# A gated cross-attention block on one core: gate and up of two token blocks by Strassen's seven products

## The reference

```python
x = x + tanh(g_xattn[0]) * xattn(layernorm(x), ctx, ctx, Wq, Wk, Wv, Wo)   # x: (2, 2048, 512), ctx: (2, 77, 512), 16 heads of 32, causal mask
x = x + tanh(g_ffn[0]) * ffn(layernorm(x))

def ffn(x):                       # HIDDEN = 1536, weights are int32 in -127..127, times 1/127
    gate = einsum('bsd,hd->bsh', x, wg)
    up = einsum('bsd,hd->bsh', x, wu)
    return einsum('bsh,dh->bsd', silu(gate) * up, wd)
```

## Time and profile before

| | |
|---|---|
| median of 3 runs | 936.83 us (935.4 to 937.76) |
| the profiled execution's own time | 934.25 us |
| its span | 932.0 us |
| mean granted TensorE clock | 0.996 of full speed |
| TensorE busy | 899.7 us, 97% |
| VectorE, ScalarE, GpSimd busy | 514.3, 349.9, 316.1 us |

### The profile page before, as it was taken

How to read it: one execution, slowest core, us unless ns; L and a number is a source line. 1 busy time by engine, 2 the same in 40 slices (tenths; PEclk the granted TensorE clock), 3 DMA queues, 4 the chain that set the end, 5 groups by cost and what they waited for, 6 DMA issues and landing times.

```text
span 932.0 us, 12820 instructions
## 1 busy us (share of the span) xinstructions
PE 899.7 (97%) x4281; PEld 745.7 (80%) x4281; DVE 514.3 (55%) x918; ACT 349.9 (38%) x999; POOL 316.1 (34%) x273
## 2 busy tenths in 40 slices
PE   5979999999999999999999999999999999999997
PEld 3757888888888887788888888888888888888886
DVE  4767867777776758587255244254262352442641
ACT  3565565556565657353033022122132131231230
POOL 5456544626272624134033032042141131231230
PEclk9989999999999999999999999999999999999999
DMA  6433424251421236730200200200100200100001
GB/s 218 125 99 107 136 65 133 76 166 49 144 79 68 79 102 195 233 115 1 71 19 12 79 0 11 79 0 23 68 0 23 68 0 34 56 0 34 12 0 47
DMA packets 48704, 65.83 MB, mean 71 GB/s; under 512 B 7328, under 2 KB 20128, under 8 KB 48672
## 3 DMA queue, kind: packets, MB, share of 16 engines
q1 hardware_dynamic: 48384, 65.41, 21.7%
q10 hardware_dynamic: 288, 0.00, 0.0%
HBM read 48.29 MB, written 16.79 MB: 70 GB/s over the span
## 4 chain that ended last, share of the span: by engine, by line
PE 84%; POOL 4%; DVE 4%; SPq 3%; issue 2%; ACT 2%; DMA 1%; POOLq 0%; ACTq 0%; DVEq 0%
PE psum L1183 61%; PE psum L1412 19%; POOL xs L488 3%; PE psum L1217 3%; SPq L378 2%; PE psum L1203 2%; POOL e L502 1%; DVE pT L828 1%; DMA wq_stage<-wq_t 1%; ACT pT L633 1%; DVE aT L844 1%; ACT aT L650 1%; ACT e L662 1%; DVE den L882 0%; SPq L310 0%
## 5 line engine op out<-in xcount | busy, mean ns | idle before, releaser
L1183 PE MATMUL psum<-xT,w_gu 128*128 128x512 f32 x1536 | 349.6, 389 | 0.0
L1183 PEld LDWEIGHTS psum<-xT,w_gu 128*128 128x128 f32 x1536 | 288.3, 188 | 59.9
L577 POOL TENSOR_TENSOR hT<-hid,hT 128x512 fp32r<-128x512 f32 x96 | 124.4, 1296 | 392.8 <-ACT hT L783 392.8
L778 ACT ACTIVATE th<-psum 128x512 f32<-128x512 f32 x96 | 57.5, 599 | 363.3 <-PE psum L1183 363.3
L1412 PE MATMUL psum<-w_d,hT 128*128 128x512 f32 x768 | 178.1, 391 | 0.0
L1412 PEld LDWEIGHTS psum<-w_d,hT 128*128 128x128 f32 x768 | 143.1, 188 | 29.1
L1068 DVE SCALAR_TENSOR_TENSOR th<-th,psum 128x512 f32<-128x512 f32 x96 | 66.0, 687 | 161.8 <-ACT th L778 161.1
L502 POOL TENSOR_TENSOR e<-e,rden 128x616 f32<-128x616 f32 x64 | 77.9, 1218 | 163.1 <-DVE rden L884 133.8
L1183 PE MATMUL psum<-xT,wq 128*128 128x512 f32 x384 | 96.4, 404 | 3.0 <-POOL xT L494 2.9
L1183 PE MATMUL psum<-wo,aT 128*128 128x512 f32 x384 | 95.9, 399 | 0.0
L1082 DVE SCALAR_TENSOR_TENSOR x<-psum,gate_ffn,x 128x512 f32<-128x512 f32 x32 | 24.0, 751 | 123.9 <-PE psum L1412 123.9
(11 more groups left out here) (81 smaller groups left out, 778.8 us busy)
## 6 DMA issues: line engine op xcount, KB each, us to landing
x_ln<-x SPq DMA_DIRECT2D x32, 256.0 KB, 4.6
x_res<-x SPq DMA_DIRECT2D x32, 256.0 KB, 3.9
x_mid<-x_res SPq DMA_DIRECT2D x32, 256.0 KB, 2.1
x<-x_mid SPq DMA_DIRECT2D x8, 1024.0 KB, 5.6
out<-x SPq DMA_DIRECT2D x32, 256.0 KB, 2.0
xs<-x_t SPq DMA_DIRECT2D x28, 256.0 KB, 3.4
raw<-w_gate_t SPq DMA_DIRECT2D x12, 256.0 KB, 3.5
raw<-w_up_t SPq DMA_DIRECT2D x12, 256.0 KB, 4.6
```

What stands on the lines that cost most here:

```text
L577: nc.gpsimd.tensor_tensor(hT[:, 1, m, :], hid[:, m % 2, :], hT[:, 0, m, :].bitcast(f32), ALU.subtract).then_inc(h_lo, 1)
L778: nc.scalar.activation(th[:, m % 2, :], psum[:, 2 * (m % 2), :], ACT.Tanh, scale=0.5 * W_SCALE)\
L1183: last = nc.tensor.matmul(dst, stat, mov, start=(j == 0), stop=(j == len(terms) - 1))
```

## The change

Two blocks of 512 rows are now taken together, as a pair p (NP = 4 pairs). For a hidden tile, gate and up of both blocks are a 2 by 2 product over halves of the 512 input columns: rows of weights A (A11, A12 of up, A21, A22 of gate) with columns of x B (B11, B21 of block 1, B12, B22 of block 2). Strassen's scheme in Winograd's form makes the four results from 7 products in place of 8. Four sums of weights S1 to S4 and four of x, T1 to T4, are needed for it. A product is 2 k-tiles by 2 parts, 4 matmuls of 128x512.

- **Weights.** During attention GpSimd turns the integers of a hidden tile into A and S (`build`, two tiles for each of six blocks) and SyncE writes them to a new tensor `w_var`. In the second stage each hidden tile's seven matrices, 128 x 1792 numbers or 0.92 MB, are loaded again for each pair into a `ring` of three slots (`load_w`). A slot is asked for again when the product p3 of its tile is done.
- **Products.** For tile i TensorE runs p1, p2, (p4 of tile i-1), p6, (p3 of i-1), p5, p7. Products p1, p6, p7 and p4 add up in one bank, and ScalarE copies the bank out between them (`snap1`, `snap2`, `snap3`); p5 and p3 share another bank.
- **Elementwise.** VectorE adds the copies to banks (`upper1` is up of block 1, `gate2` gate of block 2, `upper2` up of block 2), makes both silus (`silu1` from th1 and a bank, `silu2` from th2 and c22, both in SBUF), and silu times up of block 1 (`hidden1`, th1 and c11, both in SBUF). Silu times up of block 2 is made by GpSimd (c12 times th2). ScalarE's rounding of that, `h_high(i, 1)`, stands behind `snap1(i + 2)`, and ahead of `tanh2(i + 1)`.
- **Down** runs in two halves of 6 hidden tiles (HH): 8 row tiles by 6 by 2, 96 matmuls, after tile 6's products and again at the pair's end, and each half is added to the residual (`result`). The transposes are made from sums of x at the pair's end (`turn`), copied by ScalarE and combined by VectorE (`form`) and GpSimd.
- The pairs are written out four times in place of a loop; the threshold EXACT goes from 2^12 to 2^10.

```diff
+                    sp.wait_ge(p3_full, i + 1)
...
+                    if i + 3 < MH * NP:
+                        load_w(i + 3)
+                    if p == 0 and m == 0:
+                        for j in (4, 5):
+                            sp.wait_ge(rd_used, j - 3)
...
+                    if p == 0 and m == 2:
+                        sp.wait_ge(rd_used, HH)
+                        for j in range(2):
+                            sp.dma_start(acc[:, j * TT:(j + 1) * TT, :], mid_f[j]).then_inc(acc_in, 16)
...
+                nc.gpsimd.tensor_copy(stage[:, A21:A11].rearrange("p v k h -> p (v k) h"), raw[:, j, 0])\
...
+                pool.wait_ge(var_step, done + 5)
+                nc.gpsimd.tensor_tensor(st[S4], st[A12].bitcast(f32), st[S2].bitcast(f32), ALU.subtract)\
+                    .then_inc(var_built, 1)
...
+                build(n, 0, first)
                 probabilities(n, 3)
+                if ahead:
+                    rstd1(n + 2)
+                build(n, 1)
...
-            def h_low(n, m):
-
-                pool.wait_ge(h_hi, MH * n + m + 1)
-                nc.gpsimd.tensor_tensor(hT[:, 1, m, :], hid[:, m % 2, :], hT[:, 0, m, :].bitcast(f32),
-                                        ALU.subtract).then_inc(h_lo, 1)
...
+            def h_low(i):
+
+                for j, (h, h_hi, h_lo) in enumerate(((th1, h1_hi, h1_lo), (c12, h2_hi, h2_lo))):
+                    if j == 1:
+                        pool.wait_ge(silu2_done, i + 1)
+                        pool.wait_ge(c12_done, i + 1)
+                        nc.gpsimd.tensor_tensor(c12[:, :], c12[:, :], th2[:, :], ALU.mult).then_inc(h2_done, 1)
+                    pool.wait_ge(h_hi, i + 1)
+                    nc.gpsimd.tensor_tensor(hT[:, 1, i % HH, j, :], h[:, :], hT[:, 0, i % HH, j, :].bitcast(f32),
+                                            ALU.subtract).then_inc(h_lo, 1)
...
+                    h_low(MH * p + m)
+                    if p == 0 and m < 3:
+                        convert(2 * m)
+                        convert(2 * m + 1)
...
+            def snap2(i):
+                act.wait_ge(p6_full, i + 1)
+                if i >= 2:
+                    act.wait_ge(c12_done, i - 1)
+                nc.scalar.activation(a2[:, i % 2, :], psum[:, set_a[i % 2], :], ACT.Copy).then_inc(a2_done, 1)
...
+            def tanh2(i):
+                act.wait_ge(c22_done, i + 1)
+                if i >= 1:
+                    act.wait_ge(h2_done, i)
+                nc.scalar.activation(th2[:, :], c22[:, :], ACT.Tanh, scale=0.5 * W_SCALE).then_inc(tanh2_done, 1)
...
+                    snap1(i)
+                    if m > 1 and m != HH + 1:
+                        h_high(i - 2, 1)
+                    if m:
+                        tanh2(i - 1)
+                        tanh1(i - 1)
+                    snap2(i)
+                    if m:
+                        h_high(i - 1, 0)
+                    snap3(i)
+                    if m in (HH, MH - 1):
+                        h_high(i - 1, 1)
                 if more:
...
+            def silu2(i):
+
+                dve.wait_ge(tanh2_done, i + 1)
+                nc.vector.scalar_tensor_tensor(th2[:, :], th2[:, :], 1.0, c22[:, :], ALU.add, ALU.mult)\
+                    .then_inc(silu2_done, 1)
+
+            def silu1(i):
+
+                dve.wait_ge(tanh1_done, i + 1)
+                nc.vector.scalar_tensor_tensor(th1[:, :], th1[:, :], 1.0, psum[:, set_a[i % 2], :],
+                                               ALU.add, ALU.mult).then_inc(silu1_done, 1)
+
+            def hidden1(i):
+
+                dve.wait_ge(silu1_done, i + 1)
+                dve.wait_ge(c11_done, i + 1)
+                nc.vector.tensor_tensor(th1[:, :], th1[:, :], c11[:, i % 2, :], ALU.mult).then_inc(h1_done, 1)
+
+            def upper2(i):
+
+                dve.wait_ge(p3_full, i + 1)
+                dve.wait_ge(a2_done, i + 1)
...
+                    if m:
+                        gate2(i - 1)
+                    if m == HH + 1:
+                        first_half(p, more)
+                    upper1(i)
+                    if m:
+                        silu2(i - 1)
+                        silu1(i - 1)
+                        hidden1(i - 1)
+                        upper2(i - 1)
+                    if p == 0 and m < HH or p == NP - 1 and m >= HH:
+                        largest_gu(i)
+                gate2(last)
+                silu2(last)
+                if more:
+                    xv_low(p + 1, B11, b11_at)
+                silu1(last)
+                hidden1(last)
+                upper2(last)
...
+            def strassen(i, bank, w, v, full, start):
+
+                if i % MH == 0:
+                    xv_low_ready(pe, i // MH, v)
+                terms = [(ring[:, i % 3, w - A22, k, :], xv[:, v, a, k, :]) for k in range(KH) for a in range(2)]
...
+                    last = nc.tensor.matmul(psum[:, bank, :], stat, mov, start=start and j == 0,
+                                            stop=j == len(terms) - 1, skip_group_check=not start)
+                last.then_inc(full, 1)
...
+                pe.wait_ge(a2_done, i + 1)
+                strassen(i, set_a[i % 2], S3, T3, p7_full, False)
...
+                    p1(i)
+                    p2(i)
+                    if m:
+                        p4(i - 1)
+                    p6(i)
+                    if m:
+                        p3(i - 1)
+                    p5(i)
+                    p7(i)
+                    if m == HH:
+                        if p == 0:
+                            pe.wait_ge(rd_used, HH)
+                        for t in range(PT):
+                            down(p, 0, t)
+                if more:
+                    turn(p + 1, B11)
+                    turn(p + 1, B12)
+                p4(last)
+                p3(last)
+                down(p, 1, 0, range(HH - 1))
+                down(p, 1, 1, range(HH - 1))
+                if not more:
+                    pe.wait_ge(w_top_done, 1)
+                    pe.wait_ge(c11_done, last)
+                    nc.tensor.transpose(psum[0:1, set_b[0], 0:P], w_top[:, :], ident[:, :]).then_inc(w_top_row, 1)
+                down(p, 1, 0, range(HH - 1, HH))
+                down(p, 1, 1, range(HH - 1, HH))
+                if more:
```

More of the change, by code:

```diff
@@ L20, in flamingo_gated_block @@
     rs_row: bass.AP,
+    w_var: bass.AP,
     x_mid: bass.AP,
@@ L344, in residual @@
                     load_x(n + 2)
-                for i in between.get(-1, []):
-                    fetch(i)
+                for more in keeps[0]:
+                    keep(n - 1, 1, more)
                 for t in range(TT):
@@ L402, in _ @@
-            for i in range(3):
-                fetch(i)
-            residual(NB - 1, between={-1: [3], 0: [4], 1: [5], 2: [6], 3: [7, 8]}, mid_after=1)
-            residual(NB, between={-1: [9, 10, 11, 12], 1: [13], 3: [14]})
-            load_mid(1, 1)
-            for i in range(15, len(PARTS)):
-                fetch(i)
+                residual(n, spread=True, ahead=True, keeps=((True,), (True,)))
+            load_x2(0, 0)
+            residual(NB - 2, spread=True, keeps=((True,), (False,)))
@@ L427, in _ @@
+            for p in range(NP):
+                pair(p)
+            sp.wait_ge(out_done, 16 * PT * NP)
             with sp.If(too_wide(sp)):
@@ L592, in _ @@
+            pool.wait_ge(m_full, M_LAST + 8)
+            for p in range(NP):
+                pair(p)
             with pool.If(too_wide(pool)):
@@ L802, in _ @@
+            for p in range(NP):
+                pair(p, p + 1 < NP)
             with act.If(too_wide(act)):
@@ new lines, in first_half @@
+            def first_half(p, more):
+                for t in range(PT):
+                    if more:
+                        stats2(2 * p + 2 + t // TT, t % TT)
+                    elif t < HH:
+                        dve.wait_ge(rd_used, HH)
+                        largest(MH + t, w_d[:, 2 * t:2 * t + 2, :].bitcast(f32).rearrange("p m d -> p (m d)"))
+                    result(p, 0, t)
+                    if more and t >= PT - 2:
+                        normalise2(2 * p + 2, range(2 * (t - PT + 2), 2 * (t - PT + 2) + 2))
+                if more:
+                    normalise2(2 * p + 3)
@@ L1361, in step @@
                     o(3)
+                    turn(0, B11)
+                    turn(0, B12)
                 q(1)
```

742 lines of the change are left out of this document (456 added, 286 removed).

## The result

| | before | after |
|---|---|---|
| median, us | 935.40 (934.38 to 937.76, 5 runs) | 942.41 (942.0 to 942.9, 5 runs) |
| profiled execution: own time, span, us | 934.25, 932.0 | 942.9, 941.1 |
| mean granted TensorE clock | 0.996 | 0.985 |

The change makes the kernel slightly slower, by 0.7%: the ratio of its runs to those of before is 1.0071, with a 95% interval of 1.0055 to 1.0088. Forecast were 931.0 us, "faster" at 0.6. The time lies inside the wide range of 906 to 944, outside the forecast's own 922 to 940, and on the other side of no change.

The account below looks back on a forecast made before the run. TensorE's matmul count was taken to bound the second stage. Saved matmuls -43.5, losses +37.7 (3 x 9.0 + 8.5 + 2.2), so -5.8 on 934.25: 928.4, median 931.0 us; own range 922 to 940, wide range 906 to 944.

Parts of the forecast that it names:

- Matmuls saved: Gate and up on TensorE: 1344 matmuls in place of 1536, 192 x 0.2267 = 43.5 us less.
- Rival 2: Each product of four matmuls on TensorE pays a pause of 0.04 us, 13.4 in all: 944.4 us; chance 0.10.
- Does GpSimd hold VectorE up?: Whether `silu2` is delayed beside GpSimd's second low part; taken as yes, ring 7.18 us, 0.83 over the step.
- The upper end: Bound taken for `silu2`'s delay: it goes on only when GpSimd's low part ends, at 3.32 us in the ring.
- Rival 1: Nothing holds `silu2` up, so the elementwise ring is 6.51 us: 909.4 us at the median; chance 0.22.
- Rival 3: The weight stream comes late behind stores and residual rows, 0.45 us in some 40 steps: 949 us; chance 0.05.
- The new chain: Elementwise ring from one GpSimd product to the next: 6.51 us undisturbed, against a TensorE step of 6.35.
- How much of the ring reaches TensorE: Ring's loss left on TensorE after slack: 9.0 us a pair, 8.5 in the last pair.
- One sign: Expected in a half's trace: GpSimd's products 6.35 us apart at first and about 7.2 later.
- The seam: Last attention block to pair 0: `turn(0, B12)` waits some 2.2 us, an old wait of 1.9 goes; cost nothing.
- Edits I cost at nothing: Weight stream, `build`, writing `w_var` and the stretch before pair 0, all priced at zero.
- The loads of pair 0: Residual rows queued ahead of tile 6's weights in pair 0: weights land at 41 against a need at 39, 2.2 us.

Follow-up runs that it names:

- experiment 8: Changed kernel with silu times up of block 2 back on VectorE and pair 0's other loads later: 901.61 us, ratio 0.9631.
- experiment 1: Changed kernel with ScalarE's rounding `h_high(i - 2, 1)` moved from behind the first copy to behind the copy of p6: 922.38 us, ratio 0.9857.
- Experiment 2: Changed kernel with `silu2` reading p5's PSUM bank in place of c22, p3 waiting for it, result altered: 926.32 us, ratio 0.9896.
- experiment 3: Changed kernel with silu times up of block 2 moved from GpSimd back to VectorE: 909.31 us, ratio 0.9719.
- Experiment 9: Changed kernel with the first pair's transposes behind the last attention block's, and its block 2 statistics and normalisations moved out of the softmax: 938.22 us, ratio 1.0019.
- experiment 5: Changed kernel with the first pair's transposes and their copies behind the last attention block's last transposes: 942.06 us, ratio 1.0059.
- experiments 9 and 10: The second of the two: changed kernel with block 2's product on VectorE, pair 0's loads later, statistics and normalisations out of the softmax: 897.1 us, ratio 0.958.
- run 4: Changed kernel with pair 0's down tiles 4 and 5 and its residual rows asked for one hidden tile later: 936.72 us, ratio 1.0005.

## Why the prediction was wrong

**Right, and shown.**
- *Matmuls saved*, 43.5 us. 4089 matmuls, and with the losses taken out the kernel is 39.9 faster. Rival 2, a pause of 0.04 for each product, is refuted by experiment 8: 42.85 us for 188 matmuls are 0.23 over 188 x 0.2267, 0.005 for each of 47 products, and it needed 0.026.
- *Does GpSimd hold VectorE up?* Yes. The upper end, taken from the normalisation's rows, was the right one: expected was some 1.3 us, the median is 1.366. Experiments 1 and 2 show the cause from two sides, a `silu2` moved away from GpSimd's low part and one that reads a bank beside it, both at 0.69. The Trainium skill's rule ("SBUF — State Buffer", section "Who interferes with whom") is that two-input SBUF instructions of VectorE and GpSimd's SBUF reads exclude each other, whichever started first. The traces agree in both directions, and now with two inputs: 1.37 for 0.69 on VectorE, 1.65 and 1.74 for 1.29 on GpSimd. Rival 1, that nothing holds `silu2`, fell with it. That experiment 3 lands on its 909.4 is chance, since there another ring runs. Experiment 2, which has rival 1's ring and one wait more, takes 926.3; experiment 1, with a ring of about the same length in another order, takes 922.4, and its 13 more stand in pair 0 (15.9 over the bound, where rival 1 had 6.7), in the seam and at the start. Rival 3, a stream late in most steps, is out too: TensorE waited for it twice, in pair 0.
- *The new chain*: 7.20 measured, 7.18 worked out; 6.52 to 6.63 without the delay, 6.51 worked out (the prediction's own terms give 2.49 for `silu2`'s start and not 2.51, so 6.49).
- *How much of the ring reaches TensorE*: pairs 1 and 2 lose 10.3 and 8.9, forecast 9.0; the last 9.5, forecast 8.5. In pair 1 TensorE first waits for `a` after 128 matmuls, ahead of p7 of step 4, which is the place that the prediction had followed the slack to. One sign was off: GpSimd's products stand 7.2 apart from a half's first interval on, and not 6.35 at first; TensorE's slack hides it until step 4. The waits named for `a` and for `hT` add up to 17.2 us and not to some 38, since a good part of the loss is named nowhere (above). The whole ring was priced at 35.5 (37.7 without the loads); taking GpSimd's product out gave 33.1.

**Wrong.** The forecast of the profiled execution was 928.4 and it took 942.9, 14.5 more (the spans say 14.9: 9.1 found, -5.8 forecast). By place these 14.9 are 6.0 in pair 0, 1.3 in pair 1, 1.0 in the last pair, -0.1 in pair 2, 5.7 in the seam, 1.0 at the start. Three terms of the sum carry nearly all, two priced at nothing and one too small.
- *"The seam" was costed at nothing*, under "Edits I cost at nothing": 5.7 us. The prediction saw the wait of the second transposes for normalisations (2.2, measured 2.62) and let it be paid by an old wait that goes. It did not count VectorE's added work in the last softmax, 1.6 us in each of two row tiles, on an engine that has no time to spare there, though it is 55% busy over the kernel. Experiment 9 gives most of it back by VectorE's order, statistics and normalisations together; experiment 5 shows that the transposes' place was not it. The medians give back 4.2 and 4.5 (experiments 9 and 10); the other 1.2 to 1.5 was not taken apart, and experiment 9 has a wait of its own there (3.31).
- *The loads of pair 0*: 2.2 forecast, waits of 0.99 and 4.79 measured. The reasoning was right and the sizes were off. The residual rows are asked for at 433.31, 32.9 us into the pair and not 31, since GpSimd's three steps with conversions are 7.45 each; 3.0 MB then take until 444.01, 10.7 us and not 10.1 (0.3 of this is the prediction's arithmetic: 5.6 less 1.05 MB at 406 GB/s leaves 3.0 of latency, not 2.7); and TensorE's need came at 439.2 us, 38.8 into the pair. The 0.99 is a second wait, for tile 4's weights behind down tiles 4 and 5, and was not seen at all.
- *The clock was not priced.* In and after a long wait the granted clock was 0.50 for a while, the lower of its two levels (1.2 of 2.4 GHz), with 1.00 on both sides (below). Against the same kind of group elsewhere in after, 28 matmuls behind the wait for the stream took 2.1 us more (8.92 for 6.83), 4 matmuls and 16 transposes at the pair's end 1.6 more in pair 0 and 1.4 in pair 1 than in pair 2, 8 transposes in the seam 0.9 (1.97 for 1.03): 6.0 in all. Experiment 8 against 3 shows it for the first of these: 7.7 came back where 4.5 was waited. For the others it is read from the traces only. So some of each term above is clock, and they don't add to it.

The remaining 1.0, of the start, lies in TensorE's first wait, 0.27 longer, and in the first product with the weights' mean behind it, 8 matmuls in 6.11 us (5.26 before). It is scatter between executions more than the change: the same 8 matmuls take 5.12 us in run 2, 5.18 in run 4 and 6.68 in run 5, whose edits are all far behind them. At the median the miss is 11.4, since the execution profiled of before was 2.6 under the median of its three runs, and after's is 0.5 over.

## What to carry to other kernels

When TensorE's work shrinks, add up the ring of the elementwise engines from start to start, with the order of each list: one rounding of 0.63 us in the wrong place cost 20 us here, and no engine but TensorE was over 67% busy. A sum that leaves the forecast 6 us from no change must price every stretch that the change touches, the ones between stages first: look at whether an engine is full there, not over the span. A wait on TensorE costs more than its length where the clock goes down with it (here some 2 us behind 4.8), and when waits are short and repeated, less of the loss is named than is lost.

## What the hardware showed unexpectedly

The granted clock around the longest wait of TensorE, in after, read as windows of 2 us (clock is the third number from the right):

```profile
440.00:442.00 2.00, 0.00 (x0) 0.00 (x0) 2.00 (x3) 0.87 (x2) 1.54 (x2) 1.00 1.07 427
442.00:444.00 2.00, 0.00 (x0) 0.02 (x1) 0.04 (x1) 0.00 (x0) 0.95 (x1) 0.51 0.99 382
446.00:448.00 2.00, 2.00 (x7) 1.52 (x6) 0.20 (x1) 1.63 (x3) 0.72 (x1) 0.50 1.06 393
450.00:452.00 2.00, 2.00 (x10) 1.65 (x9) 1.89 (x3) 1.23 (x2) 0.00 (x0) 1.00 0.18 72
```

TensorE is idle from 439.2 to 444.01. The clock falls to the lower level inside this wait, stays there over the first part of the 28 matmuls that take 8.92 us, and is at 1.00 again before they end. The ends of pairs 0 and 2 have nearly the same wait (2.46 and 2.45), but in pair 0 the clock is 0.51 from 522 to 524 and in pair 2 it is 1.00 from 789 to 791. Only the first wait is followed by slow work: the transposes take 2.98 and 1.91 us, and until the next group it is 524.50 - 520.18 = 4.32 and 790.29 - 787.59 = 2.70.

```profile
520.18 1.78 PE L1753 MATMUL psum<-w_d,hT 128*128 128x512 f32 x4 [2.46 <-POOL hT L684]
521.76 2.98 PE L1570 MATMUL psum<-ident,x 128*128 128x128 f32 x16
524.50 16.60 PE L1753 MATMUL psum<-w_d,hT 128*128 128x512 f32 x72
...
787.59 1.20 PE L1753 MATMUL psum<-w_d,hT 128*128 128x512 f32 x4 [2.45 <-POOL hT L684]
788.63 1.91 PE L1570 MATMUL psum<-ident,x 128*128 128x128 f32 x16
790.29 2.08 PE L1753 MATMUL psum<-w_d,hT 128*128 128x512 f32 x8
```

In run 4 the transposes at all three pairs' ends are slow (3.44, 3.09 and 2.58 us), in run 1, whose wait there is 1.4, none is (1.91 each). It isn't the place: in runs 5 and 9 pair 1's end is the quick one and pair 2's the slow one, from wait to next group 2.70 and 4.3 us. So the pair doesn't set it, and what decides at a wait of 2.4 stayed open.

The other surprise is that the exclusion of VectorE and GpSimd costs nothing where it stands in no ring longer than the step. In run 3 it lengthens `silu2` in three steps of four and GpSimd's first low part from 1.29 to a mean of 1.74, and the TensorE waits for GpSimd's low part add up to 0.5 us, for VectorE's silu to none.
